# Turning the operands of a main matmul stage round: x stationary, the fused matrix moving in 512 columns, the bias added on GpSimd

## The reference

```
# layer 0: quantise with 8 levels of threshold, router with top 2 of 4, LoRA of rank 16
q   = for each element the dequantised value of the first group whose threshold holds it, else 0
x1  = x + sum_e gates[t, e] * (q @ A[e].T) @ B[e].T * 4
# layer 1: W with a per-batch adapter, then a kernel with bias and two adapters
y   = x1 @ W.T + 0.5 * (x1 @ lora_A[labeler]) @ lora_B_w.T
out = x1 + y @ kernel + bias + adapters(y)
```

## Time and profile before

| what | value |
|---|---|
| median of 3 runs | 496.11 us (495.85 to 497.77) |
| the profiled execution's own time | 495.29 us |
| its span, first to last instruction | 493.5 us |
| mean granted TensorE clock | 0.976 |
| busy: PE, DVE, ACT | 474.0, 390.8, 362.9 us |

### The profile page before, as it was taken

One profiled execution on the slowest core, in us unless ns is written; L12 is line 12 of the kernel. 1 busy time (PEld: TensorE's weight loads), 2 busy tenths in 40 slices (PEclk: granted clock), 3 DMA queues, 4 the chain that ended last, 5 costly groups with the idle time before them and its releaser, 6 DMA issues.

```text
span 493.5 us, 7301 instructions
## 1 busy us (share of the span) xinstructions
PE 474.0 (96%) x3000; PEld 412.5 (84%) x3000; DVE 390.8 (79%) x379; ACT 362.9 (74%) x328; POOL 7.3 (1%) x12
## 2 busy tenths in 40 slices
PE   6989999998989999999999999999999799999897
PEld 5963888886758888798998998988989789889896
DVE  2299979779979989758699899798899991997600
ACT  4879987774897496596699698966998877758002
POOL 0000000001000010000000000000000000000000
PEclk9599999999999999999999999999999799989999
DMA  8976533112402237211442317105405112101102
GB/s 277 419 250 227 151 122 104 54 47 93 106 1 85 87 96 203 76 32 39 112 139 57 94 54 234 55 1 149 139 1 150 53 44 86 54 2 44 42 1 86
DMA packets 35507, 50.21 MB, mean 102 GB/s; under 512 B 26738, under 2 KB 26994, under 8 KB 33074
## 3 DMA queue, kind: packets, MB, share of 16 engines
q1 hardware_dynamic: 34322, 41.35, 26.6%
q0 software_dynamic: 1152, 8.39, 5.0%
HBM read 38.99 MB, written 10.49 MB: 100 GB/s over the span
## 4 chain that ended last, share of the span: by engine, by line
PE 71%; DVE 14%; issue 6%; ACT 6%; DMA 2%; SPq 0%; ACTq 0%; DVEq 0%
PE bank L930 10%; PE bank L932 9%; PE bank L931 9%; DVE val L595 7%; PE bank L942 5%; PE bank L893 5%; PE bank L889 4%; PE bank L890 4%; PE bank L824 4%; PE bank L850 4%; PE bank L872 3%; ACT val L400 3%; PE bank L790 2%; DVE inside L588 2%; DMA la<-la_in 2%
## 5 line engine op out<-in xcount | busy, mean ns | idle before, releaser
L930 PE MATMUL bank<-x_hi,p_hi 128*128 128x256 f32 x512 | 155.2, 303 | 0.0
L400 ACT ACTIVATE val<-level,shift,small 128x2048 f32<-128x2048 int16 x64 | 133.9, 2091 | 16.3 <-DVE val L595 16.2
L932 PE MATMUL bank<-x_hi,p_lo 128*128 128x256 f32 x512 | 145.7, 285 | 0.0
L931 PE MATMUL bank<-x_lo,p_hi 128*128 128x256 f32 x512 | 145.7, 285 | 0.0
L595 DVE COPY_PREDICATED val<-inside,val 128x2048 f32<-128x2048 uint8 x56 | 141.9, 2535 | 0.3
L389 ACT ACTIVATE level<-xq,inv 128x2048 int16<-128x2048 f32 x64 | 127.8, 1997 | 1.8 <-DMA xq<-xt_in 1.4
L578 DVE TENSOR_SCALAR val<-val,width,unshift 128x2048 f32<-128x2048 f32 x64 | 86.1, 1347 | 26.3 <-ACT val L400 25.9
L930 PEld LDWEIGHTS bank<-x_hi,p_hi 128*128 128x128 f32 x512 | 99.1, 194 | 5.8 <-issue 4.6
L931 PEld LDWEIGHTS bank<-x_lo,p_hi 128*128 128x128 f32 x512 | 99.0, 193 | 1.1
L932 PEld LDWEIGHTS bank<-x_hi,p_lo 128*128 128x128 f32 x512 | 98.9, 193 | 0.0
L588 DVE TENSOR_SCALAR inside<-absx,thr 128x2048 uint8<-128x2048 f32 x56 | 71.5, 1287 | 7.0 <-ACT absx L381 7.0
(11 more groups left out here) (86 smaller groups left out, 461.5 us busy)
## 6 DMA issues: line engine op xcount, KB each, us to landing
xq<-xt_in POOLq DMA_DIRECT2D x8, 1024.0 KB, 6.1
xs<-xt_in SPq DMA_DIRECT2D x8, 1024.0 KB, 6.1
out_t<-ost SPq DMA_DIRECT2D x16, 512.0 KB, 3.0
wst<-w_in SPq DMA_DIRECT2D x14, 512.0 KB, 3.6
la<-la_in SPq DMA_DIRECT2D x4, 512.0 KB, 10.2
kst<-k_in SPq DMA_DIRECT2D x4, 512.0 KB, 13.7
lb<-lb_in SPq DMA_DIRECT2D x1, 2048.0 KB, 20.4
kst<-k_in SPq DMA_DIRECT2D x1, 2048.0 KB, 7.8
```

The costliest lines, as they stand in the source:

```text
L400: nc.scalar.activation(val[:, turn(c, g)], level[:, g % 2], ACT.Relu, bias=shift[:, g:g + 1], scale=par[:, 1, g:g + 1]).then_inc(raised, 1)
L930: mm(o, p_hi[:, h, k, at:at + P], x_hi[:, s, k], start=k == 0, stop=False)
L931: mm(o, p_hi[:, h, k, at:at + P], x_lo[:, s, k], start=False, stop=False)
L932: mm(o, p_lo[:, h, k, at:at + P], x_hi[:, s, k], start=False, stop=False)
```

## The change

The two sides of the main product change places. A tile is now 128 tokens (t = 0, 1) by 512 output columns (h = 0, 1), four tiles (TILES) for each batch instead of eight, and each is spread over two slots of 12 matmuls. The stationary side is a 128x128 piece of x_hi or x_lo, and P moves in 512 columns. The closing product has `zt` stationary and `tb` moving in 512 columns. `z_end` and the closing are no longer in one slot: ZEND is the slot behind whose matmuls `z_end` stands, and CLOSE is at least one slot later (for batches 5, 6, 7: z_end at main-stage slot 40, 49, 59, closing at 41, 50, 60). LAST goes from 72 to 70, so that DONE becomes 2, 7, 16, 27, 38, 49, 60, 70, mid(6) and mid(7) stand in slots 61 and 71, and the turn of batch 7 in slot 74.

ScalarE evicts 28 tiles of 128x512 by a plain copy. GpSimd adds the bias, which is now an array of 128x1024 with the same row in every partition, to 128x1024 halves of `ost`, 14 of them (7 batches), in place. The last batch's four tiles are evicted by VectorE with the bias added. The loads of `xq` for batches 4 to 7 stand between GpSimd's additions in its queue. The last matmul of a batch on x signals `x_done`, which now frees its buffers of x_hi and x_lo for the batch after next. The stores write natural layout, and the host turns nothing.

```diff
-    LAST = STEPS + BATCH * KT - 8
+    LAST = STEPS + BATCH * KT - 10
-    CLOSE = [0 if OUT_AT[b] < STEPS + b * KT else max(1, OUT_AT[b] - STEPS - b * KT) for b in range(BATCH)]
-    TAKE = [max(q + LAG, ZOUT[q // KT]) for q in range(BATCH * KT)]
+    ZEND = [max(b * KT - 1, OUT_AT[b] - STEPS) for b in range(BATCH)]
+    CLOSE = [max(b * KT + 1, ZEND[b] + 1) for b in range(BATCH)]
+    TAKE = [max(2 * q + 1, CLOSE[q // TILES]) + LAG for q in range(BATCH * TILES)]
...
+            def add_bias(b, t):
+                pool.wait_ge(ofree, STEPS + b * TILES + (t + 1) * HALVES)
+                nc.gpsimd.tensor_tensor(ost[:, t], ost[:, t], bias, ALU.add).then_inc(biased, 1)
+            for c in range(4):
+                quant_input(c)
+            pool.wait_ge(bias_in, 16)
+            asked = 4
+            for b in range(BATCH - 1):
+                for t in range(TT):
+                    while asked < BATCH and DONE[asked - 2] <= STEPS + TAKE[b * TILES + t * HALVES]:
+                        quant_input(asked)
+                        asked += 1
+                    add_bias(b, t)
...
+                    sp.dma_start(bias, a["bias"]).then_inc(bias_in, 16)
...
+                if b + 2 < BATCH:
+                    xs_load(b + 2)
+                for t in range(TT):
+                    if b + 1 < BATCH:
+                        sp.wait_ge(biased, b * TT + t + 1)
+                    else:
+                        sp.wait_ge(out_made, t + 1)
+                    sp.dma_start(out_t[b, t], ost[:, t]).then_inc(out_stored[t], 16)
...
-                        nc.scalar.activation(ost[:, m % KT], cols[m % CRING][:, 0:TOK], ACT.Identity,
-                                             bias=bias[:, m % KT:m % KT + 1]).then_inc(ofree, 1)
+                        nc.scalar.activation(ost[:, t, h * HALF:(h + 1) * HALF], cols[n % CRING], ACT.Copy).then_inc(ofree, 1)
...
+            for t in range(TT):
+                dve.wait_ge(out_stored[t], 16 * c)
+                for h in range(HALVES):
+                    n = c * TILES + t * HALVES + h
+                    dve.wait_ge(ofull, STEPS + n + 1)
+                    last = nc.vector.tensor_tensor(ost[:, t, h * HALF:(h + 1) * HALF], cols[n % CRING], bias[:, h * HALF:(h + 1) * HALF], ALU.add)
...
-                        mm(o, p_hi[:, h, k, at:at + P], x_hi[:, s, k], start=k == 0, stop=False)
+                for k in range(part * KT // 2, (part + 1) * KT // 2):
+                    mm(o, x_hi[:, s, k, at], p_hi[:, h, k], start=k == 0, stop=False)
+                    mm(o, x_hi[:, s, k, at], p_lo[:, h, k], start=False, stop=False)
+                    last = mm(o, x_lo[:, s, k, at], p_hi[:, h, k], start=False, stop=False)
+                if q in ZEND:
+                    z_end(ZEND.index(q))
+                if q in CLOSE:
...
+                    for m in range(c * TILES, min((c + 1) * TILES, (q + 1) // 2)):
+                        close(m)
+                elif part and q > CLOSE[b]:
+                    close(n)
```

More of the change, by code:

```diff
@@ L89, in build @@
     xs, xs_at = place("xs", [P, KT, TOK], F32)
-    ost, ost_at = place("ost", [P, KT, TOK], F32)
+    ost, ost_at = place("ost", [P, TT, D], F32)
     x_hi, x_hi_at = place("x_hi", [P, 2, KT, TOK], F32R)
@@ L95, in build @@
     ust, _ = place("ust", [P, 2, BATCH * R], F32)
-    ab, _ = place("ab", [3 * R, 2, D], F32R)
+    ab, ab_at = place("ab", [3 * R, 2, D], F32R)
     ab_raw, _ = place("ab_raw", [3 * R, 2, D], F32, x_lo_at)
@@ L131, in build @@
     kp_lo, _ = place("kp_lo", [P, KT, HALF], F32R, x_lo_at)
+    bias, _ = place("bias", [P, D], F32, ab_at)
     w_bytes = KT * P * 4
@@ L197, in build @@
     CRING = len(cols)
-    N_CONST = 4
+    N_CONST = 3
+    TILES = TT * HALVES
     AHEAD = 5
@@ L272, in _, with quant_input @@
         def _(pool):
-            for c in range(BATCH):
+            def quant_input(c):
                 if c == 1:
@@ L293, in _ @@
             sp.dma_start(lb, a["lb"]).then_inc(lb_in, 16)
-            for dst, name in ((bdmask, "bdmask"), (ident_raw, "ident"), (before, "before"), (bias, "bias")):
+            for dst, name in ((bdmask, "bdmask"), (ident_raw, "ident"), (before, "before")):
                 sp.dma_start(dst, a[name]).then_inc(consts_in, 16)
@@ L362, in _ @@
             for b in range(BATCH):
[L363 to L374, removed]
+                if b + 2 < BATCH:
[6 more added lines that the diff above has]
+                    sp.dma_start(out_t[b, t], ost[:, t]).then_inc(out_stored[t], 16)
+                if b + 2 < BATCH:
+                    sp.wait_ge(ofull, STEPS + (b + 1) * TILES)
+                    rows(b + 2)
+            for t in range(TT):
+                sp.wait_ge(out_stored[t], 16 * BATCH)
         @block.scalar
@@ L556, in _ @@
                         quant(c, g)
[L557 to L562, removed]
-                        nc.scalar.activation(ost[:, m % KT], cols[m % CRING][:, 0:TOK], ACT.Identity,
-                                             bias=bias[:, m % KT:m % KT + 1]).then_inc(ofree, 1)
+                for n in range((BATCH - 1) * TILES):
+                    if TAKE[n] == q:
+                        c, (t, h) = n // TILES, divmod(n % TILES, HALVES)
+                        act.wait_ge(ofull, STEPS + n + 1)
+                        if c:
+                            act.wait_ge(out_stored[t], 16 * c)
+                        nc.scalar.activation(ost[:, t, h * HALF:(h + 1) * HALF], cols[n % CRING], ACT.Copy).then_inc(ofree, 1)
                 if slot(b, j) in RANK:
@@ L752, in _ @@
                         x_part(b + 1, XAT.index(j - 1))
+            c = BATCH - 1
+            dve.wait_ge(bias_in, 16)
+            for t in range(TT):
+                dve.wait_ge(out_stored[t], 16 * c)
[3 more added lines that the diff above has]
+                    last = nc.vector.tensor_tensor(ost[:, t, h * HALF:(h + 1) * HALF], cols[n % CRING], bias[:, h * HALF:(h + 1) * HALF], ALU.add)
+                last.then_inc(out_made, 1)
         @block.tensor
@@ L914, in _, with close @@
             z_end(0)
[L916 to L922, removed]
+            def close(n):
+                c, (t, h) = n // TILES, divmod(n % TILES, HALVES)
+                mm(cols[n % CRING], zt[:, c % ZSLOTS, t * P:(t + 1) * P], tb[:, c % 2, h * HALF:(h + 1) * HALF],
+                   start=False, stop=True).then_inc(ofull, 1)
@@ L923, in _ @@
+            for q in range(BATCH * KT):
+                b, j = divmod(q, KT)
+                n, part = divmod(q, 2)
+                s, (t, h) = b % 2, divmod(n % TILES, HALVES)
+                if j == 0:
+                    pe.wait_ge(x_lo_made, (b + 1) * XPARTS)
+                if part == 0:
+                    if n < RING:
                         pe.wait_ge(ofree, STEPS)
-                    elif q < CRING:
+                    elif n < CRING:
                         pe.wait_ge(bp_made, 2 * HALVES)
@@ L941, in _ @@
[L941 to L948, removed]
@@ L953 @@
+                if slot(b, j) in MID:
+                    mid(MID[slot(b, j)])
+                if slot(b, j) in TURN:
+                    gated_turn(TURN[slot(b, j)])
+                if b + 1 < BATCH and j == ZAT:
+                    z_begin(b + 1)
 def kernel(**inputs):
```

45 lines of the change are left out of this document (21 added, 24 removed).

## The result

The changed kernel takes 503.24 us (median, 503.08 to 503.82), the kernel before in the same comparison 495.98 us (494.84 to 497.77). The ratio is 1.014 (95% interval 1.010 to 1.018): the change makes the kernel 7.3 us slower. I had forecast 492, faster. The profiled execution has a span of 501.9 us (first to last instruction) and took 503.82.

What follows compares the result with a forecast made beforehand. Three legs bound the kernel: TensorE to mid(6), VectorE's batch 7 quantiser, TensorE to the end. Batch 6 at 404, mid(6) to 407.6, batch 7 at 453.3, plus 36.3 gives span 489.6, forecast 492 us, range 482 to 507.

Steps and rivals of the forecast that it cites:

- the price of an addition: GpSimd beside VectorE: free if asked for in value or mask, 1.27 us in merge; 0.65 us each, 13 make 8.4.
- The second step: TensorE's clock in the last leg: it waits some 7 us for mid(7), and a fall of its clock is worth 1.5 us.
- the last leg: TensorE behind batch 7's quantiser: 30.0 us before, 34.8 with eight slots behind mid(7) instead of six, 36.3 with the clock.
- my sum: At mid(6): TensorE could start at 398.7, VectorE's batch 6 is done at 403, said as 404, so VectorE decides.
- Batch 7's own stretch: VectorE's quantiser of batch 7: 45.7 us less a value (1.3) plus two additions (1.3), ending at 453.3.
- The slow rival: Additions hold VectorE up for their full length, 13 x 2.3 to 2.5 us: time about 510, or 504 with pauses; chance 0.30.
- point of decision: In the full-length rival: from about 1 us for each addition it decides, the time there being that of before.
- The free rival: GpSimd's additions are free or only get VectorE's pauses: mid(6) at 399, batch 7 done at 447, 483 to 486; chance 0.22.
- the load of the bias row: 512 KB more on SP's queue among the loads of W, needed first in slot 21: costs nothing.
- ScalarE's shorter evictions: ScalarE's 64 evictions of 466 ns become 28 of 587 ns, 13.4 us less; off the chain, so counted as nothing.
- Starvation: VectorE leaves GpSimd no pause, stores come late, ScalarE waits some 5 us in two or three places: 500 us; chance 0.07.
- No closer matmuls: Main stage: wide matmuls don't come closer together, 512 columns cost twice 256; last leg loses 1.2 us, time 493.5; chance 0.05.

Runs made afterwards that it cites:

- half additions: Changed kernel with GpSimd's additions of half the size (128x512), the bias left out of the other half of the columns in batches 0 to 6: 488.03 us, one execution.
- its two variants: Kernel before with 14 GpSimd additions of the same shape put in: 511.98 us, ratio 1.033; kernel before with LAST at 70 instead of 72: 499.04 us, ratio 1.007.

## Why the prediction was wrong, point by point

**The step that failed is the price of an addition.** "So value and mask hold GpSimd up, merge does not", and an addition asked for in value or mask was to be free, because it starts with the merge. By that I put 0.65 us on each; it is 2.1. The reading came from a DMA instruction of 0.53 us that ran freely beside a merge. That instruction is no model for one that reads 128x1024 operands from SBUF: the merge that began at 283.88 took 4.75 us. And what is held up is held up for nearly the whole length of the addition, not for the overlap that was left over. The Trainium skill's rule ("SBUF — State Buffer", Who interferes with whom), which I had set beside the row and given 0.30, is borne out by the 13 additions, also for VectorE instructions with two SBUF inputs. It is not borne out by the form with one operand, which takes 2.77 us and holds up one neighbour by 0.7, and the order of first come, which I had taken from it, does not describe the addition that was passed over for eight us. My estimate of 2.2 us for this shape, from the figure of "GPSIMD Engine Reference" in the Trainium skill (Performance versus the Vector engine), stands against 2.35 us measured in a pause.

**The second step is the clock.** I had 36.3 us for the last leg, with 1.5 for the clock; it took 40.0. The run with idle matmuls has 34.3, so the wait and the clock behind it cost 5.7. I had sized it by the earlier trace rows, where TensorE had been idle for 2.75 us; here it had been idle for 5.8, and mid(7), which takes 3.79 us at the full clock, ran wholly at the lower level. At mid(6) I had counted no fall at all, and it took 5.5 us instead of 3.6.

**The miss in span** is 12.3 us: batch 7's quantiser ended at 461.9 where I had 453.3 (8.6), and the leg makes 3.7. Of the 8.6, 6.7 had built up when batch 6 was done (410.7 for 404): VectorE was busy 11 us longer than in my sum and idle 4.5 us less (10.5 for 15), 1.2 I had rounded up, and the main stage began 1.5 us later than before (202.80 for 201.29). 1.9 is mid(6). Batch 7's own stretch came out right by luck (45.6 us for 45.7): its two additions cost 4.2 us where I had 1.3, and VectorE's pauses in it, 3.3 us before, shrank to 0.5.

**The slow rival was right in mechanism and near in time** (504; 503.2), in part by luck. Its sum had batch 7 done at 471.8 instead of 461.9 and a leg 3.7 us too short, which together make 508 for a span of 501.9; the 504 came from taking off a few additions for pauses, without a count. One addition fell into a pause, and batch 7's stretch had lost its own pauses. Its point of decision, that about 1 us for each addition gives the time of before, was wrong: half additions cost 1.0 us each and the time was 488. By these two points, 1.0 us with 488.0 and 2.1 us with 503.2, I estimate it at 1.6.

**The free rival fell.** Its numbers, mid(6) at 399, batch 7 done at 447 and 483 to 486 us, can be held against the run without additions: 401.8, 446.7 and 483.0. Two errors cancel there. TensorE came to mid(6) 3.1 us behind the 398.7 of my sum. From the start of the main stage it was 14.5 us quicker than before, where my terms (distance of the matmuls, closing of batch 5, slot won) made 15.5; but the stage began 2.2 us later (203.46 for 201.29). I had put the load of the bias row at nothing. In the kernel before and its two variants the stage began between 201.3 and 202.4, in the others between 201.7 and 204.8; whether that load has part in it can't be told from these runs. And VectorE needed 41.3 us from the end of mid(6) to that of batch 7's quantiser instead of 44.4, because the pause of 2.8 us in which it had waited for ScalarE's values was gone. I had counted nothing for ScalarE's shorter evictions; that they are what closed the pause is likely but was not run by itself. Nor was the new matmul order, without the other parts of the change.

**Starvation** did not come: additions took up to 10.6 us from request to end, inside the slots that they have. ScalarE's eviction waited for TensorE 1.1 us in all and for no store. **No closer matmuls** did not come either: they start 0.227 us apart.

## What to carry to other kernels

Work given to GpSimd isn't free beside a busy VectorE. For an addition of two operands count nearly its whole length as VectorE's (here 2.1 of 2.35 us), and compare it with VectorE doing the work itself (here 0.70 us for a tile while evicting it, against 1.0 for an addition of that size). The busy engine's pauses take up the first part, here some ten us; what lies above is paid, and TensorE, which now waits, loses its clock as well. A short instruction that slips by in a trace says nothing of a long one of another kind.

## What the runs showed of the hardware that I had not expected

- An instruction of VectorE on 128x8 elements took 1.96 us in place of 0.17 beside GpSimd's addition.
- Beside a VectorE without pauses, seven additions got in at its next instruction, and four were passed over first, one of them for eight us.
- GpSimd's instruction with one operand (128x1024) took 2.77 us in a pause, longer than the addition's 2.35, and lengthened its neighbour by only 0.7 us, in three cases a second one too.
- A matmul of 64 rows between matmuls of 128 cost 0.62 us, one with 128 rows in its place 0.22 (6.96, 6.56 and 6.34 us for a tile).
- 46 idle matmuls of 256 columns in a wait of 5.8 us, together with 12 in one of 1.7, saved 5.7 us in the last leg.
